# New unit orders for five engines and a PSUM bank table in a fused four-stream transformer kernel

## The chip, the cores and the metric

The kernel runs on one core of a Trainium2 chip. The metric is the device time of one execution in microseconds; for the kernel before, three runs give a median of 3539.75 us (3533.16 to 3548.29).

## What is computed

The input is a batch of 32 sequences of 256 tokens with 128 channels, in fp32. Four blocks follow each other, and each sequence passes through them independently:

```
x = x + attention(layernorm(x))            # A0: 16 heads of 8 channels, softmax over 256 keys
x = x + relu(layernorm(x) @ w1 + b1) @ w2 + b2
x = x + attention_rope_causal(layernorm(x)) @ wo      # A1
z = layernorm(x);  x = x + local(z)        # L0, L1: two layers of
   # shift tokens, q,k,v (8 heads of 64), l2norm, xpos rotation, windowed softmax (64),
   # projection and residual, shift, layernorm, gated GELU feed-forward, residual
```

## The kernel before

The work is cut by sequence and by stage into four streams: ATTN0 (A0, first attention and its feed-forward), ATTN1 (A1), LOCAL0 and LOCAL1 (L0, L1, the two local layers). A stream is a list of units (`stream_units`, line 180): 57, 52, 51 and 52 of them, 212 in all. A unit is a small step, such as `turn_k` (two groups of PE transposes), `maxes` (scores only for the row maxima), `scores`, `mix` (probabilities times values), `qkv2`, `rope2`, `norm2` or `turn_p`. Each of five engines has its share of a unit, or none: PE the matmuls, VectorE the maxima, rotations, normalisations and some evictions of PSUM, ScalarE the exps, GELUs and other evictions, GpSimd parts of the norms and rotations and A1's masks, SyncE the transfers.

In a round each stream does all of its units once, for one sequence, or for two neighbouring ones: it begins at unit `BEGINS[k]` (line 68) and wraps. `TAKES_UP` says in which round the first sequence enters. The program has rounds 0 to 5 written out, a loop of 25 rounds (6 to 30), and rounds 31 to 36 written out. Rounds 5 and 31 are full as well; the others hold only part of the units.

The order in which an engine takes the four streams' units in a round is a string of 212 digits (`TURNS`, line 71), one for each engine; a digit names the stream whose next unit comes. Every engine works strictly in that order. A unit whose engine share is empty costs nothing at its place. Waits are on counters: each unit raises named counters, and a later unit waits for their count at its place in PE's order (`so_far`, line 410).

PSUM's eight banks are two rings of four (`RINGS`, line 108): "dense" for transposes and projections, "score" for maxes, scores, scores2 and turn_p. Each unit that uses one takes the next bank of its ring in PE's order (line 213). PE waits until the bank's last user has been evicted (`free`), the evicting engine until PE has filled it.

SyncE issues the transfers inside a round in its own order: the next sequence's load (L499, unit A0.residual), K for A0 and A1 (L508, four transfers at `turn_k` part 1), K for the local streams (L516, two transfers at `turn_k2` part 1), the token shift before the feed-forward (L522 and L523 at `shift_rows`; the second moves 256 bytes) and the store (L528 at `finish`). In the order before these are: A0.residual, L1.shift_rows, A1.turn_k, L1.finish, A0.turn_k, L0.turn_k2, L1.turn_k2, L0.shift_rows. On VectorE, `stats` of a local stream (L789) waits for its shifted rows. On PE, `maxes` part 0 and `scores2` part 0 (L1133) wait for K, and `turn_p` part 0 (L1151) for VectorE's `norm2` (L948).

## Time and profile before

| | |
|---|---|
| median of three timed runs | 3539.75 us |
| the profiled execution | 3529.4 us |
| its span | 3527.7 us |
| mean granted TensorE clock | 0.967 of full |
| PE busy | 3059.9 us, 87% |
| VectorE busy | 2544.7 us, 72% |
| ScalarE busy | 2226.6 us, 63% |
| GpSimd busy | 1580.9 us, 45% |

The profile shows one execution, recorded by the hardware. An engine's busy time is the time in which it executes instructions; PE matmuls overlap each other and their ends are modelled, so the distance from the start of one unit to the start of the next says more about a unit's cost on PE than its busy time. A number in square brackets in a row is idle time before the instruction, with the engine and line that ended it. Times in the rows count from the start of the span.

### The profile page before, as it was taken

The page shows a single profiled execution, that of the slowest core. Times are in us where ns is not written, and L with a number is a line of the kernel's source. Part 1 is how long each engine was busy: PE and PEld are TensorE (multiplying, and loading weights), DVE is VectorE, ACT ScalarE, POOL GpSimd, SP SyncE. Part 2 cuts the span into 40 slices and gives each one's busy share as a digit, 9 for nine tenths or more (in the row PEclk, how much of TensorE's full clock was granted, in tenths as well). Part 3 has the DMA queues.
Part 4 walks back from the last instruction along what each step waited for, and adds up shares of the span by engine and source line. Part 5 has one row for each costly group of instructions (what it writes and reads, how often), then busy time and mean ns, then how long its engine had stood idle before and what let it go on. Part 6 is the DMA issues. An engine that isn't in the chain of part 4 may idle for free.

```text
span 3527.7 us, 69696 instructions
## 1 busy us (share of the span) xinstructions
PE 3059.9 (87%) x20480; PEld 2171.1 (62%) x20480; DVE 2544.7 (72%) x5886; ACT 2226.6 (63%) x6084; POOL 1580.9 (45%) x1741
## 2 busy tenths in 40 slices
PE   4678999999999999999999999999999999988764
PEld 2455666666666666666666666666666666665543
DVE  3466777877877778778777787787777877866543
ACT  2345767666666676666666676666666766665532
POOL 1034444555544445555444455554444555544432
PEclk8799999999999999999999999999999999999877
DMA  2000100111110001111100011111000111100000
GB/s 66 20 20 21 24 22 23 28 27 25 25 28 22 21 22 28 27 24 26 28 22 21 22 28 27 24 26 28 22 21 22 28 27 23 28 22 16 16 14 10
DMA packets 113412, 85.69 MB, mean 24 GB/s; under 512 B 27274, under 2 KB 112692, under 8 KB 113332
## 3 DMA queue, kind: packets, MB, share of 16 engines
q1 hardware_dynamic: 113332, 84.68, 10.5%
q8 instruction: 43, 0.70, 0.1%
q14 instruction: 37, 0.30, 0.0%
HBM read 9.17 MB, written 4.19 MB: 4 GB/s over the span
## 4 chain that ended last, share of the span: by engine, by line
PE 31%; issue 26%; DVE 20%; DMA 9%; ACT 5%; POOL 5%; SPq 2%; DVEq 1%; POOLq 0%; ACTq 0%
DMA V<-XY 4%; DMA kT<-rawP 4%; PE score L1053 4%; DVE negmax L844 3%; PE dense L1118 3%; PE dense L1164 3%; DVE rawP L911 2%; PE dense L1072 2%; DVE rawP L909 2%; DVE negmax L938 2%; PE dense L1108 2%; DVE P L948 2%; PE dense L1172 2%; PE dense L1180 2%; PE score L1151 2%
## 5 line engine op out<-in xcount | busy, mean ns | idle before, releaser
L844 DVE TENSOR_REDUCE negmax<-score 128x2 f32<-128x512 f32 (+1 forms) x896 | 558.0, 680 | 51.6 <-PE score L1032 25.3
L680 ACT ACTIVATE probs<-score 128x512 f32<-128x512 f32 (+1 forms) x1024 | 497.5, 554 | 135.0 <-PE score L1053 131.9
L604 POOL TENSOR_TENSOR rawQ<-rawQ,rawP 128x512 f32<-128x512 f32 x256 | 343.3, 1341 | 197.9 <-DVE rawP L911 192.9
L560 POOL TENSOR_TENSOR veps<-moments,eps_tile 128x2 f32<-128x2 f32 x192 | 37.4, 195 | 850.1 <-DVE moments L793 850.1
L580 POOL TENSOR_SCALAR_AFFINE_SELECT probs<-probs 128x256 f32<-128x256 f32 x512 | 217.1, 446 | 443.8 <-ACT probs L680 439.6
L1053 PE MATMUL score<-qT,kT 128*128 128x256 f32 x2048 | 380.2, 306 | 35.4 <-ACT probs L680 22.0
L1108 PE MATMUL dense<-wqkv_sb,hS 128*128 128x512 f32 x768 | 369.1, 612 | 18.6 <-DVE rawC L826 16.8
L609 POOL TENSOR_TENSOR rn<-ss,minus_half 128x16 f32<-128x16 f32 x128 | 373.1, 2914 | 13.3 <-DVE ss L918 13.0
L938 DVE TENSOR_REDUCE negmax<-score 128x2 f32<-128x384 f32 (+1 forms) x384 | 221.8, 596 | 215.0 <-PE score L1135 206.0
L1053 PEld LDWEIGHTS score<-qT,kT 128*128 128x128 f32 x2048 | 280.0, 191 | 117.8 <-issue 73.7
L710 ACT ACTIVATE rawP<-score,negmax 128x128 f32<-128x128 f32 x512 | 180.2, 370 | 194.3 <-DVE negmax L938 193.1
L663 ACT ACTIVATE qT<-dense 128x512 fp32r<-128x512 f32 x256 | 140.7, 606 | 223.3 <-PE dense L1017 223.3
L1072 PE MATMUL dense<-probs,V 128*16 128x256 f32 (+1 forms) x4096 | 247.0, 357 | 5.8 <-ACT probs L680 4.2
L695 ACT ACTIVATE rawP<-dense 128x512 f32<-128x512 f32 x256 | 152.7, 596 | 124.4 <-PE dense L1108 110.1
L1032 PE MATMUL score<-kT,qT 128*128 128x512 f32 x512 | 208.4, 482 | 25.2 <-DMA kT<-rawC 13.8
L1108 PEld LDWEIGHTS dense<-wqkv_sb,hS 128*128 128x128 f32 x768 | 137.0, 194 | 144.2 <-issue 119.3
L1180 PE MATMUL dense<-rawQ,w_sb 128*128 128x256 f32 (+1 forms) x768 | 198.6, 397 | 14.6 <-DVE KB L833 9.4
L601 POOL TENSOR_TENSOR rawQ<-rawB,rope_sb 128x512 f32<-128x512 f32 x128 | 166.7, 1302 | 99.4 <-DVE rawB L925 99.4
L710 ACT ACTIVATE P<-score,negmax 128x192 f32<-128x192 f32 x512 | 209.6, 449 | 1.2 <-DVE negmax L938 1.2
L1142 PE MATMUL score<-kT,rawQ 128*128 128x384 f32 x512 | 208.0, 488 | 0.0
L1017 PE MATMUL dense<-ident_r,QB 128*128 128x128 f32 x1024 | 140.5, 282 | 74.2 <-DVE QB L853 65.0
L1017 PEld LDWEIGHTS dense<-ident_r,QB 128*128 128x128 f32 x1024 | 118.0, 145 | 119.3 <-issue 89.1
(158 smaller groups left out, 7791.2 us busy)
## 6 DMA issues: line engine op xcount, KB each, us to landing
kT<-rawC SPq DMA_DIRECT2D x256, 128.0 KB, 2.5
kT<-rawP SPq DMA_DIRECT2D x128, 256.0 KB, 3.9
xin<-x SPq DMA_DIRECT2D x32, 128.0 KB, 2.1
out<-xout SPq DMA_DIRECT2D x32, 128.0 KB, 1.8
V<-Y SPq DMA_DIRECT2D x32, 63.5 KB
V<-XY SPq DMA_DIRECT2D x32, 63.5 KB
wqkv_sb<-wqkv SPq DMA_DIRECT2D x1, 1536.0 KB
w_sb<-w SPq DMA_DIRECT2D x1, 682.0 KB
```

Of the source, the lines that this page charges most:

```text
L580: nc.gpsimd.affine_select(out=part, in_=part, compare_op=ALU.is_ge, fill=0.0, base=0, pattern=[[0, 2], [1, P]], channel_multiplier=-1)\
L604: nc.gpsimd.tensor_tensor(cosine2[:, l, n, :], cosine2[:, l, n, :], two_in_P0[:, l, n, :], ALU.add)\
L609: nc.gpsimd.tensor_tensor(rn[:, l, t].rearrange("p m h -> p (m h)"), ss[:, l, t].rearrange("p m h -> p (m h)"), minus_half[:], ALU.pow).th ...
L680: nc.scalar.activation(dst, src, ACT.Exp, scale=SCALE0 if k == ATTN0 else SCALE1)\
L710: last = nc.scalar.activation(dst, src, ACT.Exp, bias=negmax[:, k, t, hd:hd + 1], accum_out=expsum[:, l, t, hd:hd + 1])
L844: nc.vector.reduce_max(negmax[:, k, t, h0:h0 + nh], tile("score", u)[:, :].rearrange("p (h k) -> p h k", h=nh), AX.X, negate=True).then_in ...
L938: nc.vector.reduce_max(dst, src, AX.X, negate=True).then_inc(sig("max_done", u), 1)
L1017: last = turn(tile("dense", u)[:, e * SEQ + t * P:e * SEQ + (t + 1) * P], src[:, k, t, 4 * g:4 * g + 4, :].rearrange("p h c -> p (h c)"), ...
L1053: last = mm(tile("score", u)[:, i * SEQ:(i + 1) * SEQ], kT[:, k, 4 * g + 2 * e + i, t * P:(t + 1) * P], qT[:, k, g, :], start=True, stop=True)
L1072: last = mm(tile("dense", u)[32 * n:32 * n + 16, q0:SEQ], V[:, k, t, 4 * g + n, :], probs[k][t][:, n * w:(n + 1) * w], start=t == 0, stop= ...
L1108: mm(tile("dense", u)[:], hS[:, l, t * P:(t + 1) * P], wqkv2_sb[:, l, m * INNER:(m + 1) * INNER], start=True, stop=True).then_inc(has_fill ...
L1180: last = mm(tile("dense", u)[0:n, half * SEQ:(half + 1) * SEQ], w1_2_sb[:, l, half * HID + at:half * HID + at + n], hT[k], start=True, sto ...
```

## The change

The four streams begin their rounds at other units (`BEGINS`), all five strings of `TURNS` are new, and the rings are gone: a table of 166 digits (`BANKS`) gives each PSUM use, in PE's order, one of eight banks. The names and waits follow: `free`, `taken`, `uses`, `tile`, `has_filled` and `has_emptied` lose their ring argument. Waits between streams are counted by sequence (`of_sequence`) and no longer by the place in PE's order, and A1's second layernorm raises a counter of its own (`passed_on`). All eight banks are cleared at the start, where it was four. The matmuls, evictions, transfers and arithmetic of every unit are the same.

```
-BEGINS = (47, 48, 46, 30)
+BEGINS = (49, 44, 44, 22)
 TURNS = {
     "tensor": (
-        "11220233000320213133333110033031101123002322311112"
...
+        "03331331132210000222133333323333033322111111131031"
...
-RINGS = {"dense": 4, "score": 4}
+BANKS = (
+    "62643501341753610453267425301640230715234057026341"
+    "27457460326357630174267514723405171026471640254736"
+    "21504215617215310764157036472536106751204653207156"
+    "2047413071627015"
+)
+NBANKS = 8
...
-        position = {r: 0 for r in RINGS}
-        for u in self.units:
-            for r, n in u.uses.items():
-                u.buffers[r] = [(position[r] + i) % RINGS[r] for i in range(n)]
-                position[r] += n
+        banks = iter(BANKS)
+        for u in self.units:
+            u.buffers = [int(next(banks)) for i in range(u.uses)]
...
+        def of_sequence(name, k, u, pas, j, behind=0):
+            n = rises[name, k]
+            return n * (pas.first - u.stage + 1 - behind) + n * j if pas.times > 1 else n * (pas.first - u.stage + 1 - behind)
+        def began(u, pas):
+            return pas.times > 1 or pas.first > u.stage
...
-                            pe.wait_ge(raised["normed", ATTN1], so_far("normed", ATTN1, u, pas, j))
+                            pe.wait_ge(raised["passed_on", ATTN1], of_sequence("passed_on", ATTN1, u, pas, j))
```

Only the units in which an engine has work count. Read so, the new table for SyncE is: L1.shift_rows, A0.residual, A1.turn_k, A0.turn_k, L0.turn_k2, L0.shift_rows, L1.finish, L1.turn_k2. The end and the beginning of the new round on PE, and on VectorE, are:

```
PE:      ... L0.project2 L1.turn_q2 (0,1) L1.turn_k2 (0,1) A0.scores15 A1.mix2 A0.mix3
         A1.scores12..15 A0.attn_out0 | A0.attn_out1 L1.scores2 (0,1,2) A1.mix3 L1.scores2 (3,4)
         A1.attn_out0,1 L1.scores2 (5) L0.turn A1.turn A0.turn L0.up2 (0,1,2) A1.project1 L1.turn_p0 ...
VectorE: ... L0.project2 L0.shift_rows A1.mix2 A0.mix3 L0.stats A0.attn_out0 | A0.attn_out1
         A0.residual L1.scores2 (0) A0.stats L1.scores2 (1,2) A1.mix3 A0.apply L0.apply ...
VectorE: ... A1.qkv0 L1.project2 L1.shift_rows A1.qkv1 L1.stats A0.down0 A0.stats L1.apply ...
```

## Rows read from the trace of the kernel before

**Rows 1.** The page: busy us of an engine, share of the span, instructions.

```profile
PE 3059.9 (87%) x20480; PEld 2171.1 (62%) x20480; DVE 2544.7 (72%) x5886; ACT 2226.6 (63%) x6084; POOL 1580.9 (45%) x1741
```

**Rows 2.** SyncE's timeline: start, us, line, transfer, count; one steady round.

```profile
1506.79 0.40 SPq L499 DMA_DIRECT2D xin<-x  x1
1518.76 0.74 SPq L522 DMA_DIRECT2D V<-XY  x1
1519.56 2.74 SPq L523 DMA_DIRECT2D V<-XY  x1
1525.78 2.63 SPq L508 DMA_DIRECT2D kT<-rawC  x4
1538.91 0.41 SPq L528 DMA_DIRECT2D out<-xout  x1
...
1556.70 29.50 SPq L516 DMA_DIRECT2D kT<-rawP  x4
1587.04 0.73 SPq L522 DMA_DIRECT2D V<-Y  x1
1587.81 3.12 SPq L523 DMA_DIRECT2D V<-Y  x1
1607.68 0.40 SPq L499 DMA_DIRECT2D xin<-x  x1
```

**Rows 3.** Waits on PE in the round 1506.2 to 1607: total, times, longest.

```profile
PE score L1041 <- DVE negmax L844: 1.1, 1, 1.1
PE dense L994 <- DVE probs L808: 1.0, 1, 1.0
```

**Rows 4.** The same view over 25 rounds, 498 to 3020 us.

```profile
PE score L1133 <- DMA kT<-rawP: 27.5, 25, 1.2
```

**Rows 5.** Windows: length, busy us (and instructions) by engine, granted clock, DMA.

```profile
1533.10:1574.10 41.00, 34.74 (x197) 23.69 (x195) 39.15 (x70) 25.82 (x72) 30.26 (x25) 1.00 0.13 29
1574.10:1607.00 32.90, 32.90 (x295) 25.02 (x295) 20.91 (x52) 25.82 (x75) 8.86 (x15) 1.00 0.08 18
```

**Rows 6.** PE's timeline: start, us, line, operands, matmuls, idle before.

```profile
1514.13 1.45 PE L1000 MATMUL dense<-wqkv_sb,probs 128*128 128x384 f32 x4
...
1517.42 1.95 PE L1101 MATMUL dense<-w_sb,rawC 128*128 128x128 f32 x16
1519.81 2.84 PE L1108 MATMUL dense<-wqkv_sb,hS 128*128 128x512 f32 x6 [0.43 <-DVE rawC L826]
1522.49 1.04 PE L1017 MATMUL dense<-ident_r,QB 128*128 128x128 f32 x8
...
1524.37 1.10 PE L1108 MATMUL dense<-wqkv_sb,hS 128*128 128x512 f32 x2
...
1533.13 0.59 PE L1036 MATMUL score<-masks,ident_r 128*128 128x512 f32 x1
...
1561.64 0.49 PE L1133 MATMUL score<-masks,ident_r 128*128 128x512 f32 x1 [0.98 <-DMA kT<-rawP]
...
1574.07 0.33 PE L1151 MATMUL score<-ident_r,rawP 128*128 128x128 f32 x1 [0.32 <-DVE P L948]
...
1586.18 0.48 PE L1053 MATMUL score<-qT,kT 128*128 128x256 f32 x2
...
1590.31 0.39 PE L1133 MATMUL score<-masks,ident_r 128*128 128x512 f32 x1
```

**Rows 7.** VectorE's timeline of the same round.

```profile
1524.40 0.49 DVE L789 BATCH_NORM_STATS2 bn<-V 128x6 f32<-128x128 f32 x2 [0.95 <-DMA V<-XY]
...
1534.60 0.47 DVE L954 SCALAR_TENSOR_TENSOR rawA<-dense,b_sb,rawP 85x256 f32<-85x256 f32 x1
...
1572.25 1.76 DVE L948 TENSOR_TENSOR P<-P,recip 128x1536 f32<-128x1536 f32 x1
...
1586.46 0.42 DVE L887 TENSOR_TENSOR Y<-dense,Y 128x256 f32<-128x256 f32 x1 [2.85 <-PE dense L1172]
```

**Rows 8.** The page's transfers: line, count, KB each, median us to landing.

```profile
kT<-rawC SPq DMA_DIRECT2D x256, 128.0 KB, 2.5
```

More of the change, by code:

```diff
@@ L127, in attention_units @@
 def attention_units(rotary):
-    units = [Unit("turn", source="h", dense=1)]
+    units = [Unit("turn", source="h", bank=1)]
     extra = dict(rot_cos=1, rot_done=1, lo_ready=1) if rotary else {}
-    units += [Unit("qkv", t, dense=1, v_ready=1, hi_ready=1, **extra) for t in range(TT)]
-    units += [Unit("turn_q", u, dense=1) for u in range(2)]
-    units += [Unit("turn_k", u, dense=1, k_in=4 * 16 * u) for u in range(2)]
-    units += [Unit("maxes", u, score=1) for u in range(12 if rotary else 16)]
+    units += [Unit("qkv", t, bank=1, v_ready=1, hi_ready=1, **extra) for t in range(TT)]
@@ L134, in attention_units @@
+    units += [Unit("turn_q", u, bank=1) for u in range(2)]
+    units += [Unit("turn_k", u, bank=1, k_in=4 * 16 * u) for u in range(2)]
+    units += [Unit("maxes", u, bank=1) for u in range(12 if rotary else 16)]
     units += [Unit("negmax", m_hi=1, m_ready=1)]
-    units += [Unit("turn_q", u, source="with maxima", dense=1) for u in range(2)]
+    units += [Unit("turn_q", u, source="with maxima", bank=1) for u in range(2)]
     for g in range(GROUPS):
-        units += [Unit("scores", 4 * g + n, score=1, **(dict(masked=1) if rotary else {})) for n in range(2 * TT)]
-        units += [Unit("mix", g, dense=1)]
@@ L139, in attention_units @@
-    units += [Unit("attn_out", t, dense=1, rec_done=1) for t in range(TT)]
+        units += [Unit("scores", 4 * g + n, bank=1, **(dict(masked=1) if rotary else {})) for n in range(2 * TT)]
+        units += [Unit("mix", g, bank=1)]
+    units += [Unit("attn_out", t, bank=1, rec_done=1) for t in range(TT)]
     return units
 def local_units(last):
-    units = [Unit("shift", dense=1)]
-    units += [Unit("qkv2", n, dense=1, **(dict(sq_ready=1, sums=1) if n % 3 < 2 else {})) for n in range(6)]
+    units = [Unit("shift", bank=1)]
@@ L147, in rope @@
+    units += [Unit("qkv2", n, bank=1, **(dict(sq_ready=1, sums=1) if n % 3 < 2 else {})) for n in range(6)]
     def rope(u):
@@ L1147, in unit @@
                         pe.wait_ge(sig("p_ready", u), so_far("p_ready", k, u, pas, j))
-                    hd, bank = u.part, tile("score", u)
-                    for sem, count in newest(pas, j, free("score", u)):
+                    hd, bank = u.part, tile(u)
+                    for sem, count in newest(pas, j, free(u)):
                         pe.wait_ge(sem, count)
```

407 lines of the change are left out of this document (205 added, 202 removed).

## The prediction

> **What bounds the kernel now.** I read the page first [rows 1]: PE is busy 87% of the span, VectorE 72%, ScalarE 63%. The granted clock is 1.00 in the steady windows [rows 5], the 2.4 GHz level, so the clock is no part of this. An average over the span hides the rounds, so next come the queue's own instructions on SyncE [rows 2]. The load of the next sequence (L499) is issued at 1506.79 and again at 1607.68: a steady round takes 100.9 us. Such a round is done 25 times in the loop (L450), and rounds 5 and 31, written out, hold the same 212 units, so 27 rounds, 2724 us of the 3527.7 us span, are of this kind. The rest, about 804 us, is the first load and the ten rounds that are partly filled.
>
> Where does PE wait in a round? The waits of one round are small: the largest single ones are of 1.0 to 1.1 us, for VectorE's negmax and apply [rows 3], and one for the K transfer of L0. Over 25 rounds that last one comes 25 times, 27.5 us in all, none over 1.2 [rows 4]: the round repeats exactly. Cut at the units that matter [rows 5], the round has two regimes. From A1's first maxes (L1036 at 1533.13) to L0's first turn_p (L1151 at 1574.07, both in [rows 6]) are 41 us in which VectorE is busy 39.15 us: VectorE sets that stretch, PE only follows. In the 32.9 us from there to the round's end PE is busy throughout and VectorE 20.9 us. The first 27 us lie between the two. So two things can change the time: how much VectorE work lies in the saturated stretch, and whether something comes late where PE now runs unbroken.
>
> **The change part by part.** No instruction of work is added or removed; every unit has the same matmuls, evictions and transfers. One semaphore more (passed_on) and four more memsets of a bank cost nothing: they lie before the loop, beside the loads that every engine waits for, and at the cost of the longest VectorE instruction quoted here, 1.76 us [rows 7], they would add 7 us once if that cover were gone. The waits rewritten by sequence (of_sequence) ask for less than or the same as before. What counts is order, on five engines, and the banks.
>
> *Banks.* Before, a scores or maxes unit could be four such units ahead of its eviction. In the saturated stretch PE waits for negmax evictions (1.1 us in the waits of a round [rows 3]). Eight banks let it run further ahead, but VectorE still needs its 39 us. The stretch ends with data, not with a bank: L0.turn_p0 comes 0.06 us after the end of P (1572.25 + 1.76 in [rows 7]). So I cost the bank table by itself at 0, with -1.1 us a round as its other end.
>
> The Trainium skill ("Perfetto Trace Analysis", Matmuls) says that independent matmul groups should rotate through different PSUM banks so that evictions overlap the next group. That speaks for the table; by it the 1.1 us would go and the sum below would be some 30 us lower. The trace bears it out only in part: the stretch still ends with P.
>
> *VectorE's order in the saturated stretch.* I listed VectorE's units from A1.maxes0 to L0.norm2 (part 1) in both tables. The new list has six units fewer: L1.up22 and L1.down20 come before it, and A1.mix0, L1.scale20, L1.rope22 and L1.norms21 behind. The first of them takes 0.47 us (L954, 1534.60 [rows 7]); rope2 has two instructions, the others one, seven in all of like or smaller operands but for one of twice the size: 3.0 us, an estimate from that row. PE's list for the stretch also shrinks: it loses L1.down2, A1.mix1 and four scores and gains one qkv2 and three scores. A qkv2 takes 0.89 us (1519.81 to 1522.49 for three); eight scores and two mixes take 4.13 us (1586.18 to 1590.31 [rows 6]), so I put a score at 0.28, a mix at 0.8 to 1.0 and down2, twelve small matmuls against down0's 1.95 us for sixteen (row 1517.42), at 1.3 to 1.4. That is 1.5 us less, to be done elsewhere. Net: 3.0 - 1.5 = 1.5 us a round gained, bounds 0 (if the stretch is then held by ScalarE's exps) and 3.0 (if PE fits the moved work into idle time).
>
> *SyncE's order at the round's end.* This is the largest term. Before, L1's K transfer is the second half of the four L516, done on SyncE by 1586.20, ahead of L0's shifted rows (L522, L523 from 1587.04), and L1.scores20 (L1133) starts at 1590.31 with no wait [rows 2, 6]. In the new table SyncE has L0.shift_rows, then L1.finish, then L1.turn_k2 (part 1), and the next round begins with A0.attn_out1 and L1.scores20. On PE the new order is L0.project2, L1's four turns, A0.scores15, A1.mix2, A0.mix3, A1.scores12 to 15, A0.attn_out0, A0.attn_out1, L1.scores20. Take t = 0 at the start of the PE unit after L0.project2 (1586.18 [rows 6]). VectorE's residual ends at 1586.88 [rows 7], the first row transfer is issued at 1587.04, and the second, of 256 bytes, holds SyncE 3.12 us, until 1590.93 [rows 2]: t = 4.75. L1.finish has a transfer of 0.41 [rows 2] and its waits, together an estimated 0.75: t = 5.5. From the first L516 to PE's use of K are 4.94 us (1556.70 to 1561.64, a wait that the DMA ended [rows 2, 6]): t = 10.45. What PE has to do meanwhile, start to start: before, eight scores and two mixes took 4.13 us (1586.18 to 1590.31); now there are the two mixes and five scores, 0.85 less, the four turns, 1.88 (1522.49 to 1524.37 for four of the same form), and two attn_out of the same eight transposes, 0.8: 5.95 us [rows 6]. That leaves 4.5 us; I estimate that 0.4 us of it go into A0.mix3's wait for its exps, which stand on ScalarE behind the four turns (before, no wait of this kind comes there). Cost: +4.1 us a round. Bounds: +1.5, if other waits of PE in that piece grow to 3 us and so hide it, and +4.5. Behind the waiting L1.scores20 stand all of PE's units; VectorE at that point is blocked as well, since L0.stats (rows_in) now stands before A0.attn_out0 and needs 5.6 us from the first issue, as L1.stats does before (1518.76 to 1524.40 [rows 2, 7]).
>
> The next load (L499) moves behind L1.shift_rows on SyncE. Counted from the rows before it would be issued at 1522.3 and landed, with the 2.5 us of a K part [rows 8], by 1525.2; A0.stats, its reader, comes after L1.stats and A0.down0, at some 1525.9: 0. GpSimd, which now has A1's first eight masks after L1's second rotation and `finish` before L0's, is busy 30.3 of the 41 us [rows 5]; its new order costs 0, and up to +1.0 if a rotation comes late, which the range has room for.
>
> *The first half.* In the new order L1.project2 is followed closely by L1.stats on VectorE, which now stands before A0.down0 instead of behind it and A0.stats. From A1.qkv0's matmul (1514.13) to L1's rows in place (1524.40) are 10.3 us; then two stats, a residual and an apply, seven short instructions and two of them again as long as the 0.49 us pair of bn_stats (1524.40 [rows 7]), about 2.7 us, and 0.2 to PE, make 13.2 us to L1.turn. PE's units between are 10.3 us: A1.qkv, a turn and project2 3.29 (1514.13 to 1517.42), less the turn's 0.2 and with A0.up0's 0.9; down0 1.95; four qkv2 3.57; two turn_q 0.9 [rows 6]. A wait of 2.9 us. Before, this part of the round cost 1.0 (apply [rows 3]) and 0.43 (in row 1519.81 of [rows 6]), 1.4 in all. A1's K transfer takes, from the end of turn_k1 on PE (1524.37), until the fourth issue at about 1527.8 (1525.78, 2.63 for four [rows 2]) and 2.5 us to land [rows 8], 5.9 us. PE's work between turn_k1 and A1.maxes0 is about 5.9 us in the new table (L1.down20 in it, three qkv2 and a turn out of it), where it was 7.4; and on ScalarE A0.turn now stands ahead of A1.turn_k: +1.0 (0 to 1.4). Together 2.9 + 1.0 - 1.4 = +2.5, bounds -1.0 and +2.9. Last, L1.turn_p0 follows L1.scores25 by fewer units, with VectorE's norm2 (its longer half 1.76 [rows 7]) between, and A1.accept on ScalarE now has VectorE's apply of z shortly ahead of it: 0 to +2.0, I take +0.5, near the lower end, since PE can run ahead on eight banks there.
>
> *Sum.* +4.1 + 2.5 + 0.5 - 1.5 = +5.6 us a round, 106.5 us; times 27 is 151 us. The ten partly filled rounds I leave at 0 (-20 to +20): fewer streams share the engines, but the chains of one stream stay the same. Against the profiled execution's 3529.4 us this gives 3680 us. The median of the three timed runs, 3539.75, lies 10 us above that execution; I don't add it, the estimate is coarser.
>
> **Rivals.** *Faster, by interleaving.* If SyncE's order doesn't decide, because the rows' second transfer is short when it isn't in that place, or because PE's order gets to L1.scores20 later than the units suggest, the gains are left: 1.5 us from the stretch, the 1.4 us of waits in the first half and the 1.1 at L1133 [rows 4] gone: some 3.3 to 4 us a round, 90 to 108 us, about 3430 us. For it speaks that the new order spreads VectorE's work more evenly and mixes two streams' maxes; against it that the two L523 hold SyncE 2.74 and 3.12 us, far more than their 256 bytes would need [rows 2]. It decides if the wait at L1133 stays under about 1.5 us. The Trainium skill ("Perfetto Trace Analysis", Optimization Strategy) states that a kernel whose most contended engine changes over time can gain from interleaving those regimes; that would be this result, and [rows 5] show just such regimes. *Nothing.* The SyncE wait is about 2 us, the first half costs nothing more, and the 1.5 us pay for most of it: within 0.5%, about 3540. The variant that the change does not do what it says belongs here: the table only renames banks, since the stretch is ended by data. *Worse.* All ends meet (+4.5, +2.9, +2.0, 0), 9.4 us a round, 3783 us.
>
> **How the numbers follow.** The forecast's case, slower by the SyncE queue, has 0.50 (3600 to 3750). Faster by interleaving 0.24 (3420 to 3520), nothing 0.13, worse 0.07 (above 3750), and 0.06 for a small loss between 3560 and 3600. A measurement of this kernel tells about 0.5% from no change. Faster by more than that 0.25, within it 0.12, slower 0.63. The range must reach to the faster case: 3450 to 3750 leaves out some 0.1 below and 0.07 above. The likeliest case alone has 3600 to 3750.
>
> **What would show it.** Right: rounds of 105 to 108 us between two L499; one wait of 3.5 to 4.8 us on PE, for the DMA of kT from rawP, at L1's scores20; on SyncE the order L522, L523, L528, L516; VectorE idle up to 3 us before the bn of V from Y; the stretch from A1's maxes to L0's turn_p at about 38 us. The first half is wrong if PE's wait before L1's turn is under 1 us; the bank part is wrong if PE still waits for negmax over 1 us. The whole is wrong if the wait at L1133 is under 1.5 us in the steady rounds.

## The result and the profile after

The changed kernel takes 3838.57 us, median of four runs (3803.67 to 3855.25), the kernel before in the same comparison 3537.76 (3533.16 to 3548.29): a ratio of 1.083, 95% interval 1.079 to 1.088. The forecast was 3680, with a range up to 3750: right in sign, too small by half. The profiled execution of the changed kernel has a span of 3801.9 us, 274 us over the 3527.7 of before; it is the fastest of its four, and what follows is read from it.

From its page, the span and the busy line of the engines; the mean granted clock is 0.942 of full, where it was 0.967.

```profile
span 3801.9 us, 71578 instructions
PE 3121.8 (82%) x20480; PEld 2249.1 (59%) x20480; DVE 2533.6 (67%) x5890; ACT 2193.5 (58%) x6084; POOL 1687.5 (44%) x1741
```

VectorE has the work of before (2534 us busy, [rows 1] has 2545) and a smaller share: nothing was added to it, it waits more. PE shows 62 us more busy time though its instructions are the same 20480, the first sign of a lower clock. The load of the next sequence repeats every round (all instructions of its line from 1400 to 1800):

```profile
L516 SPq DMA_DIRECT2D xin<-x x4: 402/404/405, 1412.3 to 1740.1; - x4
```

Three rounds in 327.8 us: 109.2 to 109.3 us each, where [rows 2] has 100.9. Summed from the first matmul of each round, the 27 full rounds take 2953 us (before 2722) and the ten partly filled ones 818 (before 775; some 31 us ahead of the first matmul and behind the last are left out): 231 and 43 us, together the 274.

What SyncE issues in one round (start us, duration us; L516 is the load, L525 and L533 K, L539 and L540 the two row transfers, L545 the store; they answer L499, L508, L516, L522, L523 and L528 of [rows 2]):

```profile
1517.69 0.75 SPq L539 DMA_DIRECT2D V<-XY  x1
1518.49 2.75 SPq L540 DMA_DIRECT2D V<-XY  x1
1521.59 0.40 SPq L516 DMA_DIRECT2D xin<-x  x1
...
1590.84 0.74 SPq L539 DMA_DIRECT2D V<-Y  x1
1591.63 2.63 SPq L540 DMA_DIRECT2D V<-Y  x1
1594.64 0.40 SPq L545 DMA_DIRECT2D out<-xout  x1
1595.36 1.31 SPq L533 DMA_DIRECT2D kT<-rawP  x2
```

And PE's timeline there (L1149 and L1151 are L1.scores20, as L1133 and L1135 of before):

```profile
1590.07 1.04 PE L1134 MATMUL bank<-ident_r,rawA 128*128 128x128 f32 x8
...
1594.93 1.04 PE L1096 MATMUL bank<-ident_r,rawC 128*128 128x128 f32 x8
1600.35 0.79 PE L1149 MATMUL bank<-masks,ident_r 128*128 128x512 f32 x1 [4.38 <-DMA kT<-rawP]
1600.93 1.91 PE L1151 MATMUL bank<-kT,rawQ 128*128 128x256 f32 x4
1602.28 0.99 PE L1149 MATMUL bank<-masks,ident_r 128*128 128x512 f32 x1
```

L1's K is issued last, 5.3 us after PE has begun the unit behind L0.project2 (1590.07), and PE waits 4.38 us for it; in [rows 6] L1133 at 1590.31 starts with no wait. PE's largest waits of this round (total us, times, longest):

```profile
PE bank L1149 <- DMA kT<-rawP: 6.0, 2, 4.4
PE bank L1010 <- DVE V L824: 2.9, 1, 2.9
PE bank L1057 <- DVE negmax L860: 1.8, 1, 1.8
```

Then what the forecast had left out. The windows around that wait (length, PE busy, granted clock, DMA share, GB/s):

```profile
1595.97:1600.30 4.33, 0.00 (x0) 1.00 0.56 127
1600.30:1604.00 3.70, 3.65 (x9) 0.54 0.00 0
1604.00:1608.00 4.00, 4.00 (x30) 1.00 0.00 0
```

PE did nothing for 4.3 us, and behind it the granted clock is at its 1.2 GHz level for 3.4 us: L1.scores20 to 22 take 4.8 us, start to start, where the kernel before, at 1.00, takes 2.7: 2.1 us more. From 600 to 3000 us the trace has 45 such stretches, about two a round; the other one mostly lies among A1's maxes, behind the wait of 1.8 us for negmax. The kernel before has none from 600 to 3000 us ([rows 5] show 1.00).

The stretch in which VectorE was the bound, from A1.maxes0 to L0.turn_p0 (length, then busy us of PE, weight loads, VectorE, ScalarE, GpSimd, then clock, DMA share, GB/s):

```profile
1535.35:1574.65 39.30, 33.60 (x167) 22.75 (x168) 35.98 (x62) 24.07 (x68) 23.12 (x19) 0.96 0.12 27
```

[rows 5] has 39.15 us of VectorE in 41.0.

### The profile page after: what moved, and what is told of

Its sections match the earlier page's. It is cut to its first block, busy times and chain, and to the rows that moved or that the text cites. A ratio compares the mean times of both kernels' runs of the same rounds, so it can differ in the third digit from the quotient of the medians.

```text
span 3801.9 us, 71578 instructions
## 1 busy us (share of the span) xinstructions
PE 3121.8 (82%) x20480; PEld 2249.1 (59%) x20480; DVE 2533.6 (67%) x5890; ACT 2193.5 (58%) x6084; POOL 1687.5 (44%) x1741
## 4 chain that ended last, share of the span: by engine, by line
issue 27%; PE 21%; DVE 18%; DMA 11%; POOL 9%; ACT 9%; SPq 4%; DVEq 1%; POOLq 0%; ACTq 0%
DVE negmax L860 5%; DMA kT<-rawP 4%; DMA V<-XY 4%; PE bank L1069 3%; POOL rn L625 3%; DVE rawA L941 3%; DMA kT<-rawC 2%; DVE rawP L927 2%; ACT rawP L726 2%; PE bank L1134 2%; SPq L525 2%; PE bank L1188 2%; PE bank L1088 2%; PE bank L1151 1%; PE bank L1124 1%
## 5 line engine op out<-in xcount | busy, mean ns | idle before, releaser
L860 DVE TENSOR_REDUCE negmax<-bank 128x2 f32<-128x512 f32 (+1 forms) x896 | 557.9, 682 | 70.2 <-PE bank L1048 36.0
L696 ACT ACTIVATE probs<-bank 128x512 f32<-128x512 f32 (+1 forms) x1024 | 482.5, 577 | 136.8 <-PE bank L1069 133.1
L1124 PE MATMUL bank<-wqkv_sb,hS 128*128 128x512 f32 x768 | 392.6, 622 | 34.7 <-ACT rawA L713 32.6
L954 DVE TENSOR_REDUCE negmax<-bank 128x2 f32<-128x384 f32 (+1 forms) x384 | 225.2, 600 | 255.9 <-PE bank L1151 240.4
L1069 PE MATMUL bank<-qT,kT 128*128 128x256 f32 x2048 | 326.1, 299 | 34.2 <-ACT P L726 10.1
L1069 PEld LDWEIGHTS bank<-qT,kT 128*128 128x128 f32 x2048 | 266.1, 191 | 115.3 <-issue 39.7
L1149 PE MATMUL bank<-masks,ident_r 128*128 128x512 f32 x128 | 90.7, 708 | 202.5 <-DMA kT<-rawP 202.5
L1088 PE MATMUL bank<-probs,V 128*16 128x256 f32 (+1 forms) x4096 | 240.0, 357 | 8.8 <-ACT probs L696 7.2
L1048 PE MATMUL bank<-kT,qT 128*128 128x512 f32 x512 | 222.7, 514 | 29.5 <-DMA kT<-rawC 22.6
L726 ACT ACTIVATE P<-bank,negmax 128x192 f32<-128x192 f32 x512 | 208.8, 429 | 16.4 <-DVE negmax L954 16.4
L711 ACT ACTIVATE rawP<-bank 128x512 f32<-128x512 f32 x256 | 152.7, 597 | 100.4 <-PE bank L1124 61.6
L1158 PE MATMUL bank<-kT,rawQ 128*128 128x384 f32 x512 | 207.9, 488 | 0.0
```

The lines of the kernel that those rows point to most:

```text
L696: nc.scalar.activation(dst, src, ACT.Exp, scale=SCALE0 if k == ATTN0 else SCALE1)\
L726: last = nc.scalar.activation(dst, src, ACT.Exp, bias=negmax[:, k, t, hd:hd + 1], accum_out=expsum[:, l, t, hd:hd + 1])
L860: nc.vector.reduce_max(negmax[:, k, t, h0:h0 + nh], tile(u)[:, :].rearrange("p (h k) -> p h k", h=nh), AX.X, negate=True).then_inc(has_emp ...
L954: nc.vector.reduce_max(dst, src, AX.X, negate=True).then_inc(sig("max_done", u), 1)
L1048: last = mm(bank, qT[:, k, g, t * P:(t + 1) * P], kT[:, k, 4 * g + 2 * e:4 * g + 2 * e + 2, :], start=True, stop=True)
L1069: last = mm(tile(u)[:, i * SEQ:(i + 1) * SEQ], kT[:, k, 4 * g + 2 * e + i, t * P:(t + 1) * P], qT[:, k, g, :], start=True, stop=True)
```

## The experiments

The theory: the order of SyncE's queue makes L1's K late, PE waits, and that wait is most of the loss. Rivals: the bank table costs; the loss comes from the order on the compute engines; a wait only changes its place. After the traces a second theory stood beside the first: a long wait of PE costs a second time, by the low clock behind it.

### One unit moved on SyncE, in the kernel before

```
# TURNS["sync"] of the kernel before: L1.turn_k2 behind L0.shift_rows
-        "11133333311332222220022222222111113333300200000131"
+        "11133333311322222200222222223111113333300200000131"
```

> The kernel before, with one unit moved on SyncE alone: L1.turn_k2 (its K transfer) behind L0.shift_rows, as in the changed kernel; nothing else. Forecast's theory: K is issued at the end of the second row transfer, 5.0 us before PE can use it, so that PE starts L1.scores20 at 1596.1 where it was 1590.31: a wait of about 5.8 us a round, and 2.1 us more if the granted clock falls behind it: 5.8 to 7.9 us a round, 3695 to 3750 us against 3538. Rival B (the order of SyncE's queue is not what counts, other engines shift the work): under 2 us a round, under 3590.

Measured 3782.09 us, ratio 1.070 (1.069 to 1.072). SyncE, PE and the windows of PE behind the wait:

```profile
1578.00 0.74 SPq L522 DMA_DIRECT2D V<-Y  x1
1578.79 2.80 SPq L523 DMA_DIRECT2D V<-Y  x1
1581.92 1.31 SPq L516 DMA_DIRECT2D kT<-rawP  x2
```

```profile
1586.61 0.79 PE L1133 MATMUL score<-masks,ident_r 128*128 128x512 f32 x1 [5.16 <-DMA kT<-rawP]
```

```profile
1586.50:1590.00 3.50, 3.39 (x8) 0.50 0.00 0
1590.00:1593.00 3.00, 3.00 (x8) 0.57 0.00 0
```

One digit moved in one engine's order costs the kernel before 250 us, where the whole change costs 301: rounds of 109.2 us instead of 100.9. Of the 8.3 us a round 5.2 are the wait and 2.9 are what L1.scores20 to 23 take more than in the kernel before, at the low clock behind the wait. The forecast's mechanism holds, with a price that it had not named. The time lies above the 3695 to 3750 us expected: the wait is shorter than the 5.8 us put down for it, the low clock dearer than 2.1, and by subtraction some 26 us lie outside the 27 full rounds. How much of the change's own 301 us hangs on this queue is another question, which the runs with the changed kernel answer below.

### The wait parted from the clock

The same kernel, with matmuls in the place of the idle time. They change nothing that is kept, since the unit's own first matmul starts the bank anew.

```
                 elif u.kind == "scores2":
                     needs = [free("score", u)]
+                    if u.part == 0 and k == LOCAL1:
+                        for sem, count in newest(pas, j, free("score", u)):
+                            pe.wait_ge(sem, count)
+                        for i in range(20):
+                            mm(tile("score", u)[:], ident_r[:], band0.unsqueeze(1).broadcast_to([P, 4, P]), start=True, stop=True)
                     if u.part == 0:
                         pe.wait_ge(sig("k_in", u), ...)
```

> The kernel before with L1's K transfer moved behind L0's rows on SyncE (by itself 3782 us, a wait of 5.2 us and rounds of 109.2), and now 20 matmuls of the mask ahead of that wait, in the bank that is about to be filled: some 4.8 us of work where PE was idle. It parts the wait from the low clock behind it. Theory A (the low clock is a cost of its own, 2.9 us a round, by what L1.scores20 to 23 took more): rounds of 106.1 to 106.4, some 3700 us. Rival B (only the wait counts, the clock is no cause): 3782.

Measured 3699.68 us (3698.54 to 3700.62), ratio 1.047 (1.045 to 1.049), rounds of 106.4, as theory A has it. K comes no earlier, issued 3.9 us after the first row transfer in both; the granted clock from 600 to 3000 us is the difference (first the kernel without, then with the matmuls):

```profile
600.00:3000.00 2400.00, 2110.30 (x14070) 0.97 0.10 23
```

```profile
600.00:3000.00 2400.00, 2208.51 (x14864) 1.00 0.10 23
```

From 600 to 3000 us the kernel without the matmuls has 22 low stretches, one a round and all behind this wait; with them it has 4. So 82 us, 2.8 a round, are the low clock, and PE's idleness is its cause. A wait of 5.2 us costs 8.3 us. The Trainium skill ("TensorE: Matmul & The Clock Gate", HAM oscillation — how this bites in real kernels) describes just this: a kernel that waits for a DMA in every iteration finds TensorE at the low clock each time, and loses half of the time that is spent at it. These two runs agree: some 6.1 us a round are worked at the low clock (the two windows above), and 2.8 us are lost. Not every wait is followed by a low clock, though, as the next runs show.

### The changed kernel with its waits filled

The same matmuls in the changed kernel: 16 ahead of L1.scores20's wait, then also 11 ahead of the wait before L1's turn.

> The changed kernel, with 16 matmuls of the mask ahead of L1.scores20's wait for K, in the bank that it is about to fill (they are overwritten): PE is busy for about 3.8 of the 4.4 us in which it was idle. Theory A: the granted clock fell to 0.50 for 3.41 us behind that idle time, because of it, and L1.scores20 to 22 took 2.1 us more than L0's; with the wait filled the clock stays at 1.00 there and the round falls from 109.2 to about 107.1, the whole by some 57 us to 3780. Rival B: the low clock has nothing to do with the idle time: 3838, or some us more by the added matmuls.

> The changed kernel with both long waits of PE filled: 16 matmuls of the mask ahead of L1.scores20's wait for K (by itself 57 us less) and 11 ahead of the wait before L1's turn, each in the bank that is about to be filled. The waits stay as long as they were, only PE is busy in them. Theory A (the order costs its waits, the forecast's +5.6 us a round, and the low clock behind them is the rest of the measured +8.3): the granted clock stays near 1.00 and the round comes to 105.8 to 107, about 3740 us. Rival B (the low clock comes from the stretch in which VectorE is the bound, and costs elsewhere): no further gain against 3782.

Measured 3781.57 us (ratio 1.070, 1.068 to 1.073) and 3757.48 us (1.063, 1.061 to 1.065), against the changed kernel's 1.083. By the medians the first gain is the 57 us expected and both together are 81 us, some 17 short of what was expected. The first one's trace is less clean: the low clock behind L1.scores20's wait is gone, but behind the wait of 2.9 us before L1's turn, which the changed kernel's trace shows followed by a low stretch in four rounds from 600 to 3000 us, one now stands in 19. In that span the low stretches go from 45 to 35 to 16. Of the last 16, 14 stand among A1's maxes, where PE waits for VectorE. The profiled executions lie only 21 us apart (3780.8 against 3801.9), so the size in this kernel rests on medians of a kernel whose own runs spread over 52 us. The kernel pair above is the better measure.

### The bank table by itself

The orders of before in the code of the changed kernel, with a table made for them.

```
-BEGINS = (49, 44, 44, 22)
+BEGINS = (47, 48, 46, 30)
# TURNS of the kernel before; BANKS = "27350164257135064217502436175024316..."
```

> The orders and BEGINS of the kernel before, in the code of the changed one, with a table that gives each unit a bank of eight (for each unit the bank that was free longest, by the times of the trace of before). It tells the bank table and the waits by sequence from the order. Forecast's theory: the table by itself is worth nothing, 3538 us, or up to 1.1 us a round less, 3508. Rival (the table costs, since evictions of two engines now wait for one another): up to half of the 300 us, 3690.

Measured 3555.37 us, ratio 1.006 (1.004 to 1.008): 0.6% slower, not faster; its runs (3547 to 3559) and those of the kernel before beside them (3526 to 3541) don't overlap. Rounds without a low stretch take 100.4 us, some 0.4 less than before; most have one or two and take 101.8 to 102.4. The waits of PE over two rounds, kernel before first, then this one:

```profile
PE dense L1017 <- DVE QB L853: 4.2, 4, 1.5
PE score L1041 <- DVE negmax L844: 2.2, 2, 1.1
PE score L1133 <- DMA kT<-rawP: 2.2, 2, 1.2
PE dense L994 <- DVE probs L808: 2.1, 2, 1.0
```

```profile
PE bank L1033 <- DVE QB L869: 7.2, 4, 1.9
PE bank L1149 <- DMA kT<-rawP: 4.1, 2, 2.1
PE bank L1010 <- DVE probs L824: 3.4, 2, 1.7
```

The wait for negmax is gone, which fits the Trainium skill ("Perfetto Trace Analysis", Matmuls) and its advice to rotate through banks; the time did not fall by it. PE runs further ahead and meets the same data later in one piece: from 600 to 3000 us it has some 185 waits where it had some 265, and they are longer (2.1 us for K where 1.2 was the longest), with 26 low stretches where there was none. That the longer waits bring the low clock is argued here from their place in the trace; no run of this table has them filled. The table being free, as the forecast had it, is refuted. The counterpart, the new order with two rings of four, was not tried. In the changed kernel's trace up to seven units of the score kind are filled and not yet emptied at once, four in the kernel before, so with rings of four PE would have to wait at such places.

### K ahead of the rows, or on another queue

```
# e1: TURNS["sync"] of the changed kernel: L1.turn_k2 ahead of L0.shift_rows
-        "22222223333333333333333333333333333330000000000000"
+        "22222233333333333333333333333333333320000000000000"
```

```
# e7: ScalarE, behind the eviction of turn_k2 (and not on SyncE for this stream)
+                    if k == LOCAL1 and u.part == 1:
+                        for sem, count in newest(pas, j, taken(earlier(pas, u, "turn_k2", 0)), taken(u)):
+                            act.wait_ge(sem, count)
+                            ...
+                        for e in range(2):
+                            nc.scalar.dma_start(kT2[half, l, :, e, :], ...).then_inc(sig("k_in", u), 16)
```

> The changed kernel, with SyncE's order at the round's end turned round: L1.finish and L1.turn_k2 (K transfer) ahead of L0.shift_rows. K can then be issued when its turn is evicted, by some 1592.7 instead of 1595.36; with the 5.0 us from issue to use PE starts L1.scores20 at 1597.7: the wait falls from 4.4 to 1.7 us and the granted clock stays at 1.00 behind it (2.1 us). L0's rows are issued some 3.2 us later, and L0.stats stands on VectorE ahead of A0.attn_out. Theory A (the forecast's: the wait for K decides, VectorE absorbs the late rows): 4.8 us a round less, about 3700 us against 3838. Rival B (the late rows block VectorE, which then delays the evictions of A0.attn_out and L1.scores2; the loss only changes its place): within 1% of 3838.

> The changed kernel, with L1's K transfer (two transfers) issued by ScalarE right behind the eviction of L1.turn_k21, on its own queue, instead of by SyncE behind the rows and the output. Theory A (SyncE's queue makes K late): issued at about 1592.6 instead of 1595.36, the wait falls from 4.4 to about 1.5 us, the granted clock stays at 1.00 (2.1 us): 5 us a round less, about 3703 us; ScalarE is held some 1.3 us by the issues, in a stretch where it has room. Rival B (as with the exchanged row transfers, whatever is issued behind the 63.5 KB row transfer is slow, on any queue): issue or landing take 2 to 2.5 us longer, and the wait stays over 3.5 us: over 3790 us.

K ahead of the rows: 3899.13 us, ratio 1.103 (1.101 to 1.105), 61 us worse than the change itself. The wait for K is 2.0 us (1.7 expected), but the waits of PE over 1500 us show what took its place:

```profile
PE bank L1149 <- DVE probs L881: 58.7, 14, 4.3
PE bank L1149 <- DMA kT<-rawP: 48.0, 27, 2.0
```

PE waits 4.3 us for a bank that VectorE has not emptied, because L0.stats stands ahead of A0.attn_out on VectorE and waits for the late rows. That is rival B, and more: both transfers are urgent at this point, and one queue serves them one behind the other.

K from ScalarE's queue: 3735.41 us, ratio 1.055 (1.052 to 1.058), 103 us less than the change, 135 expected. Its largest waits beside that for V over the same 1500 us (this kernel's lines lie eight further down, so L1157 is the L1149 above; the 28 waits are L0's and L1's):

```profile
PE bank L1157 <- DMA kT<-rawP: 39.4, 28, 1.7
PE bank L1096 <- ACT probs L704: 20.8, 14, 1.5
```

The 4.4 us are gone, and so is the low clock at L1.scores20; a new wait of 1.5 us for ScalarE, which is held 1.27 us by the two issues, takes much of the difference. In the changed kernel too the queue makes K late. But mended alone this way it gives back 103 of the 301 us, where 4.4 + 2.1 us in 27 rounds would be 176, and the trace still has 28 low stretches from 600 to 3000 us, 13 of them behind the wait of 2.9 us before L1's turn. So the theory that this wait is most of the loss holds for the one digit in the kernel before; for the change as a whole it is shown for a third.

### L1's turn later

L1's turn moved on PE and ScalarE behind L0.qkv24, A1.turn_k0 and turn_k1, units keeping their banks; then the same with K from ScalarE.

```
# PE:  L0.qkv23 L1.turn(gained) L0.qkv24 A1.turn_k0 A1.turn_k1 A0.turn
# ->   L0.qkv23 L0.qkv24 A1.turn_k0 A1.turn_k1 L1.turn(gained) A0.turn
```

> The changed kernel, with L1's turn (L1010 behind the rows of V from XY) moved behind L0.qkv24 and A1.turn_k0, turn_k1 on PE and ScalarE, every unit keeping its bank. PE has 1.7 us more work ahead of the turn. Theory A (the forecast's first half: PE waits 2.9 us for the chain of L1's residual, rows and norm, and nothing else): the wait falls to about 1.2, A1's K comes 1.7 us earlier as well: 1.7 us a round less, 3792 us against 3838. Rival B (VectorE sets the time from there on, the saturated stretch begins no earlier): within 0.3% of 3838.

> The last two edits together in the changed kernel: K of L1 from ScalarE's queue, and L1's turn later. If both waits cost what they last, and add: 6.7 us a round, about 3657 us. If they share a cover (VectorE is then the bound earlier), 3 to 5 us a round, 3700 to 3757 us.

Measured 3943.37 us (1.116, 1.114 to 1.117) and 3806.59 us (1.077, 1.075 to 1.078): both expectations failed. The edit costs the changed kernel 105 us, and 71 where K comes from ScalarE. The wait for V is 0.9 us now, but a line stands beside it that the changed kernel has at 0.2 us:

```profile
PE bank L1196 <- ACT rawQ L649: 33.1, 26, 2.3
PE bank L1010 <- DVE V L824: 11.7, 13, 0.9
```

The three units were the cover for the eviction of that turn on ScalarE, ahead of L1.up20. Moved ahead of the turn they leave it bare, behind ScalarE's other evictions, and a low stretch of 6.8 us now begins there, at A0.turn or behind it, and covers L1's up2 units in nearly every round (21 from 600 to 3000 us). A wait can't be filled with the units that cover the next one.

### The row transfer

Why is the issue of 256 bytes so long? First the two transfers exchanged, then whole rows (1 KB pieces, half as many, twice the bytes) in both kernels and with K from ScalarE. With whole rows VectorE's copy of the half that isn't shifted moves behind its wait for the rows.

```
-  sp.dma_start(h[k][1:P, :, 64:DIM], Y[l][0:P - 1, :, 64:DIM])
+  sp.dma_start(h[k][1:P], Y[l][0:P - 1])          # VectorE writes columns 0:64 again afterwards
```

> The changed kernel, with the two row transfers of shift_rows exchanged: the one of 256 bytes is issued first, the one of 63.5 KB second. In the changed kernel the second one holds SyncE 2.63 and 2.75 us, the first 0.75. Theory A (the forecast's: what holds SyncE belongs to the small transfer being second, and both waits of PE hang on it): the pair takes about 1.2 us instead of 3.4, L1's K transfer is issued 2.3 us earlier, PE's wait before L1.scores20 falls from 4.4 to about 2.1 and the granted clock stays at 1.00 behind it (another 2.1 us), the wait before L1's turn falls from 2.9 to under 1: some 6.7 us a round, about 3655 us against 3838. Rival B (the time belongs to the place, whatever comes second is slow): the pair still takes 3.4 us and the time stays within 0.5% of the changed kernel. Rival C (the waits hang on something else): the pair is short, and the time still stays at 3838.

> The changed kernel, with the row transfer in other pieces: whole rows of two times 128 elements, 127 pieces of 1 KB instead of 254 of 256 bytes, and VectorE copies the half that isn't shifted over it afterwards (it did so before, in parallel). Theory A (the number of small pieces is what makes the issue behind this transfer take 2.4 to 2.7 us): the issue behind it takes under 1 us, L1's K transfer is issued some 2 us earlier, the rows land 1 to 2 us earlier; waits of 4.4 and 2.9 us fall to about 2.4 and 1.5, the clock stays at 1.00 behind the first: 5 us a round less, about 3700 us against 3838. Rival B (the hold is not one of pieces, or the rows' landing is the longer end): under 2 us a round, over 3780.

> The same edit of the row transfer in the kernel before, where K of L1 is issued ahead of the rows and PE has cover for L1's chain. Theory A (there the rows are hidden behind VectorE's and PE's other work; VectorE idles 1.4 us a round for them): between 0 and 1 us a round less, 3510 to 3538. Rival B (VectorE's copy is now on the chain and costs): up to 3555.

> The changed kernel with both edits of the transfers: whole rows, and L1's K from ScalarE's queue, which by itself gave 3735 us. If the rows' landing is shorter, the wait of 2.9 us before L1's turn falls to about 1.5: 3695 us. If the landing is the same, 3735 us as without it.

Exchanged: 3811.98 us, ratio 1.081 (1.077 to 1.085), no change beyond the spread of the runs: the pair is short, as rival C has it, and nothing is gained. SyncE then shows the small transfer at 0.58 us, the large one at 0.73, and the store behind them long:

```profile
1593.60 0.58 SPq L539 DMA_DIRECT2D V<-Y  x1
1594.22 0.73 SPq L540 DMA_DIRECT2D V<-Y  x1
1595.32 2.45 SPq L545 DMA_DIRECT2D out<-xout  x1
1598.10 1.31 SPq L533 DMA_DIRECT2D kT<-rawP  x2
```

So it is neither the small transfer nor the second place: whatever is issued behind the transfer of 127 rows is held.

Whole rows: 4083.52 (1.156, 1.154 to 1.157), 3699.09 in the kernel before (1.047, 1.045 to 1.048) and 4085.70 us (1.156, 1.154 to 1.158): much worse. In the changed kernel with whole rows, an issue of SyncE and a line of VectorE's waits over 1500 us:

```profile
1580.28 1.05 SPq L540 DMA_DIRECT2D V<-Y  x1
```

```profile
DVE V L801 <- DMA V<-Y: 61.5, 12, 5.1
```

The hold fell from 2.6 us to 1.1, near what theory A had: the number of pieces has a part in it. But VectorE waited 5.1 us for the rows, and the time went the other way in all three; nothing had been expected to lose as much. The moved copy takes 0.23 us, too little to be the reason. What was left was in the DMA lines of the changed kernel, 1590 to 1600 us in 40 slices (busy tenths of 16 engines, then GB/s):

```profile
DMA  0000000000000000000110692019999799992000
GB/s 0 0 0 0 0 0 0 0 0 13 17 18 18 18 17 18 14 17 18 19 19 17 199 286 66 8 45 205 180 172 180 127 217 287 332 287 66 0 0 0
```

The rows flow at 18 GB/s for over 3 us, the store and K behind them mostly at 130 to 330. The last experiments cut the 127 partitions (the counter `rows_in` then waits for three transfers).

```
-  sp.dma_start(h[k][1:P, :, 64:DIM], Y[l][0:P - 1, :, 64:DIM]).then_inc(sig("rows_in", u), 16)
+  sp.dma_start(h[k][1:113, :, 64:DIM], Y[l][0:112, :, 64:DIM]).then_inc(sig("rows_in", u), 16)
+  sp.dma_start(h[k][113:P, :, 64:DIM], Y[l][112:P - 1, :, 64:DIM]).then_inc(sig("rows_in", u), 16)
```

> The changed kernel, with the row transfer of 127 partitions cut into one of 112 and one of 15, in the same pieces of 256 bytes. In the trace of the changed kernel the transfer of 127 partitions flows at 17 to 19 GB/s for 3.5 us, one DMA engine of 16 busy, where the K and output transfers flow at 180 to 330 GB/s; with whole rows, twice the bytes, it took still longer (VectorE waited 5.1 us for it). Theory A (127 partitions go over one DMA engine, 112 over several, and that is both the late rows and the issue held 2.7 us behind it): the rows land some 2.5 us earlier, the issue behind takes under 1 us, K is issued 1.5 to 2 us earlier; the wait of 2.9 us before L1's turn falls to about 0.5, that of 4.4 before L1.scores20 to about 2.5, the clock stays at 1.00 behind them: 6 to 7 us a round less, 3650 to 3680 us against 3838. Rival B (the pieces of 256 bytes are slow on any number of engines): within 1% of 3838.

> The same cut of the row transfer in the kernel before. There VectorE idles some 1.4 us a round for the rows of V from XY, and PE has cover. Theory A: 0 to 1 us a round less, 3510 to 3538. Rival B (the rows set more of the round than the waits show, as the 1 KB rows, 164 us slower, would suggest): 2 us or more a round less, under 3485.

> The changed kernel with the cut rows and L1's K from ScalarE's queue (by itself 3735 us). If the two waits are then both gone and the order has a gain of its own in the stretch where VectorE is the bound (39.3 us where it was 40.95): a round of 99 to 101 us, 3500 to 3560 us, level with the kernel before or ahead of it. If the order costs elsewhere: over 3600 us.

> The kernel before with the row transfer cut into 112 and 15 partitions (by itself 3500 us, rounds of 99.96), and L1's K transfer moved behind it on SyncE. The rows hold the queue 2.3 us where they held it 3.5, so K is issued about 1.5 us earlier than with the uncut rows: a wait of 3.7 us instead of 5.2. Theory A (the order of the queue costs its wait whatever the rows take, and the low clock follows): 103.6 us a round without and 106.5 with a low clock, 3600 to 3680 us. Rival B (it was the slow row transfer alone that made the order costly): under 3550.

Changed kernel with cut rows: 3690.34 us, ratio 1.044 (1.042 to 1.046), 148 us less, 10 short of the 3650 to 3680 expected. Its SyncE rows and its DMA line (1547 to 1557 us in 40 slices):

```profile
1547.50 0.63 SPq L539 DMA_DIRECT2D V<-Y  x1
1548.17 0.95 SPq L540 DMA_DIRECT2D V<-Y  x1
1549.17 0.62 SPq L541 DMA_DIRECT2D V<-Y  x1
1550.16 0.40 SPq L546 DMA_DIRECT2D out<-xout  x1
1550.90 1.32 SPq L533 DMA_DIRECT2D kT<-rawP  x2
```

```profile
GB/s 0 0 0 0 0 0 0 143 86 0 0 31 0 1 1 0 166 291 68 0 25 193 180 180 164 147 172 279 324 307 127 0 0 0 0 0 0 0 0 0
```

The 112 rows now go at up to 143 GB/s and are over in half a microsecond (two slices of 0.25 us); nothing behind them is held for more than 0.95 us, K is issued 3.40 us after the first row transfer instead of 4.52, and PE waits 3.3 us for it (4.4). The wait before L1's turn falls from 2.9 to 0.7. The Trainium skill ("DMA: Bandwidth & Descriptors", Why a DMA increments its semaphore by 16 and not by 1) has the reason: the number of DMA engines that a transfer uses is the largest one up to 16 that divides the size of its outermost dimension, on both sides, and 127 partitions go over one; by it 112 go over 16. The measured rates agree, 18 GB/s for 127 partitions and 143 for 112. The hold goes with the pieces: 254 in the transfer of 127 partitions 2.6 us, 127 pieces 1.1, and 224 pieces in that of 112 partitions 0.95. That fits a hold set by how many pieces one DMA engine gets, and not by their number alone; these three transfers differ in bytes too, so it is not shown apart.

With K from ScalarE as well: 3652.93 us, ratio 1.032 (1.029 to 1.034), where 3500 to 3560 was hoped for. Both long waits are then gone (0.7 us before L1's turn, no wait for K over 1.7), and the new order still takes 103.3 to 106.1 us a round, 104.7 in the mean: no gain of its own shows. What is left of its loss is seen as waits of 1 to 2 us and the low clock behind some; no run parts the new order of PE from that of VectorE or ScalarE. The cut rows in the kernel before: **3499.56 us, ratio 0.990 (0.989 to 0.992), faster than both kernels**, with rounds of 100.0 us; its five runs (3492 to 3508) all lie under those of the kernel before beside them (3532 to 3544). That is between the two theories (3510 to 3538, under 3485). What falls is PE's wait for A0.apply, which stands on VectorE behind L1.stats and its wait for the rows, from 600 to 3000 us in the kernel before and in this one (whose lines lie one further down):

```profile
PE dense L994 <- DVE probs L808: 24.9, 24, 1.1
```

```profile
PE dense L995 <- DVE probs L809: 4.7, 24, 0.2
```

So the new order with both edits must be held against 3499.56, and is 153 us, 4.4%, slower. And K moved behind the cut rows there: 3678.69 us, ratio 1.041 (1.040 to 1.043), the upper end of what was expected, a wait of 3.9 us and rounds of 105.9. The slow transfer made this order of the queue dearer (250 us), but it isn't the whole loss: with fast rows the order still costs 179 us.

## Why the prediction was right and wrong, point by point

- *What bounds the kernel.* The two regimes, the exact repetition and the 27 rounds held. One reading was off: PE's longest single wait in a round is 1.5 us, for VectorE's QB (L853, shown with the bank table), and not 1.0 to 1.1. "The clock is no part of this" failed. It was read from a kernel whose PE never stands still for more than 1.5 us in these rounds, and then kept for one in which the forecast itself put a wait of over 4 us. **This is the step that failed**: no term of the sum stood for a low clock behind that wait, and it costs 2.1 us a round behind L1.scores20 (2.9 where K alone was moved), 57 us in 27 rounds. It is the largest part of the 124 us between the forecast and the profiled execution (3803.67), but not all of it: the partly filled rounds are 43 and the stretch where VectorE was the bound 35, both below; the other terms nearly cancel. The median lies another 35 us higher.
- *Banks, 0 or -1.1.* Wrong in sign, small in size: 0.6% slower alone. In the changed kernel PE still waits 1.8 us for negmax, which by the forecast's own mark refutes the bank part. The term had 0 for its upper end and should have had a cost there.
- *VectorE's order, -1.5.* VectorE's part was sized well: its load in the stretch fell by 3.2 us (forecast 3.0). PE's busy time there fell by 1.1, with a low stretch of the clock in it (forecast 1.5 from the units' times). But the stretch shortened by 1.7 us only, to 39.3 where 38 was forecast: against the 1.5 us of work moved out of it a net 0.2 a round. With 36.0 us of VectorE in 39.3 it is no longer the bound throughout; waits of PE for negmax, rawA, rawB and K, and a low stretch of the clock, lie in it. Which of them holds it was not separated.
- *SyncE's order, +4.1.* Right, nearly to the tenth, where t = 0 is the start of the PE unit behind L0.project2: K issued at t = 5.3 (forecast 5.5), used at 10.3 (10.45), PE there at 5.9 (5.95), a wait of 4.4. Only the 0.4 that A0.mix3 was to take didn't come. That the queue's order makes this wait is shown by three runs (K alone moved; K from ScalarE; K alone behind cut rows), the low clock's share of its price by the fourth (the wait filled).
- *First half, +2.5, and turn_p, +0.5.* The wait before L1's turn is 2.93 us (forecast 2.9), by the chain that the forecast named. PE's waits up to A1.maxes0 come to 4.2 us (2.93, 0.74, 0.32, 0.22) where they were 1.8 (1.03, 0.43, 0.33): +2.4. That this meets the 2.5 is partly luck: A1's K costs 0.3 instead of 1.0, and a wait of 0.7 for VectorE's rawA ahead of L1.down20 takes its place. turn_p costs nothing. Outside the stretch the round is 10.0 us longer (69.9, was 59.9); less the 1.5 us of work moved there, the 4.4 and the clock's 2.1, a remainder of 2.0 is left for all of this, where 3.0 was forecast.
- *The next load and GpSimd, 0.* Right: the load is issued 8.6 us after A1.qkv0's first matmul (forecast 8.2, from 1514.13 to 1522.3), and no wait of PE ends on either.
- *Sum.* With the measured sizes: 4.4 + 2.1 (clock) + 2.0 - 0.2 = 8.3 us for a common round; the mean over the 27 is 8.6, since a few rounds have a longer low stretch or a third. Without the clock the forecast's 5.6 would have met 6.2. Of the signs that were to show it right, the wait of 3.5 to 4.8 us, SyncE's order and VectorE's idle time before the bn of V from Y (2.1 us) came; the rounds of 105 to 108 us (109.2) and the stretch of 38 (39.3) didn't.
- *Partly filled rounds, 0 (-20 to +20).* They cost 43 us. That the same waits occur wherever both of the streams concerned run is the likely reason, not measured here; some of the per-round cost should have been carried over to them.
- *Rivals.* "Worse" (3783, chance 0.07) came nearest, by ends that didn't meet: it had 9.4 us a round and no clock in it. "Faster by interleaving" was to decide itself at a wait under 1.5 us; with both waits largely gone (3653 us) the order is still 3% slower than the kernel before, and 4.4% slower than that kernel with the same cut rows, so its gain isn't there.

## What to carry to other kernels

Cost a new wait of PE twice: its length, and, where the clock falls behind it, about half of the time worked at the low clock (2.9 us of 6.1 in one kernel here, 2.1 of 3.4 in the other, which is more than half). A change that gathers short waits into a long one can lose even at an equal sum. Walk every queue in the order of issue, with what each transfer holds up behind it. A transfer on 127 partitions is slow itself and holds the next issue, and cutting it into 112 and 15 was worth 1% to the kernel before and 4% to the changed one. Before filling a wait with units from behind it, ask which wait they cover now. A cause that is worth 250 us in one kernel can give back only 103 in another: hold each edit against the kernel that it is made in.

## What was unexpected of the hardware

- An issue behind the transfer of 127 partitions in 254 pieces is held 2.4 to 2.8 us, and 2.9 to 3.8 us (medians) where K goes out beside the rows or just ahead of them, whatever is issued; behind 127 pieces 1.1 us, behind 112 partitions 0.95 us, with that transfer landing in 2.0 to 2.1 us in the changed kernel.
- The low clock follows waits shorter than expected, and not by their length alone. In the changed kernel the wait of 1.8 us for negmax, in a stretch where PE is idle now and then, is followed by one in 19 of the loop's 25 rounds, and the longer one of 2.9 us before L1's turn in 5. Of which idleness it takes the runs don't tell.
- Kernels of different work have rounds of the same length: 109.2 us in the changed kernel, with the rows exchanged, with K alone moved, and with the turn later and K from ScalarE; 105.8 to 105.9 with cut rows in the changed kernel and with K behind cut rows. All have low stretches. Why is open. It also means that an edit's waits and its time need not move together: with the rows exchanged the trace has 22 low stretches from 600 to 3000 us instead of 45, and the round is as long.
- The changed kernel's runs spread over 52 us, those of before over 15. The granted clock goes with it: 0.942 in the run of 3804 us, 0.930 in those of 3848 and 3855. In the one traced, rounds 22 to 25 take 110.3 to 111.2 us; from 23 to 26 the second low stretch stands behind the wait before L1's turn. The spread may be how often that happens; the traces don't show it.
